# Graph network on one core: part of a histogram moved to ScalarE, one node stage reordered, another that makes its rows with TensorE

## What is computed

```python
x = _layernorm(x + _L2_gnn_ref(x, ...))          # its end: x1 = ln(x + agg); ln(x1 + gelu(x1 W1.T + b1) W2.T + b2)
def gat_conv(x, W, att_src, att_dst, b, src, dst):
    h = (x @ W).reshape(n, H, C)
    a_s = jnp.einsum('nhc,hc->nh', h, att_src)
    a_d = jnp.einsum('nhc,hc->nh', h, att_dst)
    ...                                          # softmax over each node's edges and the node itself
    out = jax.ops.segment_sum(h[s] * alpha[:, :, None], d, num_segments=n)
    return out.reshape(n, H * C) + b
h = gat_conv(x, W1, att_src1, att_dst1, b1, src, dst) + x @ Wsk1 + bsk1
h = jax.nn.relu(h)
out = gat_conv(h, W2, att_src2, att_dst2, b2, src, dst) + h @ Wsk2 + bsk2
```

## Time and profile before

| what | value |
|---|---|
| median of 3 runs | 4936.54 us (4929.94 to 4939.66) |
| the profiled execution: time, span | 4934.43 us, 4932.7 us |
| granted TensorE clock, mean over the span | 0.868 |
| PE, DVE, ACT, POOL busy | 3297.2, 3312.0, 2347.0, 3364.9 us |
| first walk | 71 to 378 us |
| third node stage | 2420 to 3164 us |
| fourth node stage | 3735 to 4209 us |

### The profile page before, as it was taken

One profiled execution on the slowest core, in us unless ns is written; L12 is line 12 of the kernel. 1 busy time (PEld: TensorE's weight loads), 2 busy tenths in 40 slices (PEclk: granted clock), 3 DMA queues, 4 the chain that ended last, 5 costly groups with the idle time before them and its releaser, 6 DMA issues. The chain is left out here.

```text
span 4932.7 us, 95098 instructions
## 1 busy us (share of the span) xinstructions
PE 3297.2 (67%) x20852; PEld 2470.8 (50%) x20853; DVE 3312.0 (67%) x13416; ACT 2347.0 (48%) x6751; POOL 3364.9 (68%) x4041
## 2 busy tenths in 40 slices
PE   0888868888886999767499999630005999321666
PEld 0776757777563444322267777420004777211665
DVE  6987874444785777789588888641805888624676
ACT  0556767767674444333288888400002444000566
POOL 3746757677455777457588888775674555674999
PEclk9999989999998999889799999855557999655888
DMA  4447869889897422101144444351116998441676
GB/s 96 150 142 234 256 194 265 245 253 266 255 284 246 149 53 52 30 28 39 63 143 145 145 145 145 109 152 41 37 41 210 293 294 270 113 111 51 194 224 199
DMA packets 592049, 784.40 MB, mean 159 GB/s; under 512 B 138298, under 2 KB 361838, under 8 KB 591298
## 3 DMA queue, kind: packets, MB, share of 16 engines
q1 hardware_dynamic: 430208, 532.17, 35.4%
q0 software_dynamic: 62848, 112.43, 9.4%
q10 hardware_dynamic: 98822, 138.05, 7.6%
HBM read 470.04 MB, written 317.95 MB: 160 GB/s over the span
## 5 line engine op out<-in xcount | busy, mean ns | idle before, releaser
L2895 POOL TENSOR_SCALAR n_hot<-node_of,d_krel 128x256 f32<-128x256 f32 x396 | 381.1, 978 | 65.2 <-ACTq L2951 65.2
L1374 ACT ACTIVATE n_r<-n_r,n_shift,n_rstd 128x128 f32<-128x128 f32 x784 | 321.6, 481 | 70.6 <-POOL n_shift L1365 65.7
L2923 PE MATMUL n_bank<-h_rows,n_hot 128*128 x1584 | 240.6, 320 | 145.7 <-POOL n_hot L2895 128.7
L2923 PEld LDWEIGHTS n_bank<-h_rows,n_hot 128*128 128x128 f32 x1584 | 228.2, 231 | 158.7 <-issue 158.6
L684 POOL DMA_INDIRECT agg<-e_whole,e_put_i x196 | 202.7, 1034 | 149.5 <-DVE e_whole L714 90.1
L1374 ACT ACTIVATE n_o<-n_y_ps,n_shift,n_rstd 128x128 f32<-128x128 f32 x784 | 292.7, 453 | 13.5 <-POOL n_shift L1645 13.1
L970 POOL DMA_INDIRECT by_src<-by_src_pay,by_src_place_i x196 | 207.7, 1060 | 116.4 <-DVE n_o L1552 59.5
L1000 POOL DMA_INDIRECT x_rows<-x,d_other_i x196 | 191.4, 976 | 117.6 <-POOLq L102 58.2
L615 POOL DMA_INDIRECT agg_dst<-e_rows,e_put_i x196 | 195.2, 996 | 102.0 <-issue 59.4
L2516 POOL TENSOR_TENSOR n_u<-n_u 128x512 f32<-128x512 f32 x98 | 124.5, 1270 | 205.4 <-DVE n_u L2463 205.4
L2645 POOL DMA_INDIRECT h_rows<-h,d_other_i x196 | 201.3, 1027 | 76.2 <-issue 59.4
(11 more groups left out here) (510 smaller groups left out, 11343.1 us busy)
## 6 DMA issues: line engine op xcount, KB each, us to landing
n_ag<-agg_dst SPq DMA_DIRECT2D x196, 264.0 KB
n_hs<-h SPq DMA_DIRECT2D x196, 264.0 KB
n_xs<-x SPq DMA_DIRECT2D x196, 256.0 KB, 4.2
agg_dst<-e_ev SPq DMA_DIRECT2D x196, 132.0 KB
y<-n_o ACTq DMA_DIRECT2D x98, 264.0 KB, 3.6
e1a_fed<-y SPq DMA_DIRECT2D x196, 132.0 KB
m<-e1a_ev SPq DMA_DIRECT2D x196, 132.0 KB
e1b_fed<-m SPq DMA_DIRECT2D x196, 132.0 KB
```

The source lines that it names most:

```text
L1374: ins = act.activation(out[:, g, 0:D], r[:, g, :], ACT.Identity, bias=shift[:, g:g + 1], scale=rstd[:, g:g + 1])
L2895: ins = pool.tensor_scalar(hot[:, i // STEPB % HOTS, i % STEPB, :], keep.node_of[:, :], e.krel[:, i:i + 1], None, ALU.is_equal)
L2923: ins = pe.matmul(bank[:, bass.ds(to + h * 256, SUMMED)], hot[:, s, k, h * P:(h + 1) * P], flat_rows[:, bass.ds(row, SUMMED)], start=False ...
```

## The change

Three edits, with no edge between them but the chain of stages.

First, the last 76 of the 196 digits are counted by ACT: the sum over a partition's edges of sign(key + level), once for each level, and the difference of two neighbouring sums, halved, is a count. DVE counts 120, and takes the differences.

```diff
+    def count_signs(self, act):
+        act.wait_ge(self.digits_found, 3)
+        for d in range(BY_SIGN):
+            if d >= FOUND:
+                act.wait_ge(self.signed, d - FOUND + 1)
+            act.activation(self.sign_of[:, d % FOUND, :], self.beside[:, HIGH:HIGH + J], ACT.Sign, bias=self.level[:, d:d + 1],
+                           accum_out=self.signs[:, d:d + 1]).then_inc(self.signed, 1)
...
-        for d in range(HIGH):
+        for d in range(HIGH - BY_SIGN):
...
-        dve.wait_ge(self.counted, HIGH)
+        dve.wait_ge(self.signed, BY_SIGN)
+        dve.wait_ge(self.counted, HIGH - BY_SIGN)
+        self.link(dve.tensor_tensor(self.hist[:, HIGH - BY_SIGN:HIGH], self.signs[:, 0:BY_SIGN], self.signs[:, 1:BY_SIGN + 1], ALU.subtract))
+        self.link(dve.tensor_scalar(self.hist[:, HIGH - BY_SIGN:HIGH], self.hist[:, HIGH - BY_SIGN:HIGH], 0.5, None, ALU.mult))
```

Second, the loops of the third node stage are written in another order, and `add_beta` runs two blocks later:

```diff
-                pipeline(pool, (4, deviation(1, sums2, rstd2)), (5, deviation(2, sums3, rstd3)), (1, deviation(0, sums1, rstd1)),
-                         (1, add_beta))
+                pipeline(pool, (3, add_beta), (4, deviation(1, sums2, rstd2)), (5, deviation(2, sums3, rstd3)),
+                         (1, deviation(0, sums1, rstd1)))
...
-                         (0, together(0, sums1)), (4, second_residual), (3, statistics(1, y_ready, lambda s: y_ps[s % BANKS])),
-                         (4, statistics(2, residual, lambda s: r2[:, s % 2])), (3, together(1, sums2)), (4, together(2, sums3)))
+                         (3, statistics(1, y_ready, lambda s: y_ps[s % BANKS])), (4, second_residual), (3, together(1, sums2)),
+                         (4, statistics(2, residual, lambda s: r2[:, s % 2])), (0, together(0, sums1)), (4, together(2, sums3)))
...
-                pipeline(pe, (2, turn1), (7, product3), (6, turn3), (3, ffn2), (2, ffn1))
+                pipeline(pe, (7, product3), (2, turn1), (6, turn3), (3, ffn2), (2, ffn1))
...
-                pipeline(act, (3, gelu), (2, move1), (5, third_norm), (6, move3), (1, first_norm), (7, keep_h))
+                pipeline(act, (3, gelu), (2, move1), (7, keep_h), (6, move3), (5, third_norm), (1, first_norm))
```

```diff
-        sp.dma_start(self.hs[:, s], block_rows(h, turn, s)).then_inc(self.h_in[s], 16)
...
-                pipeline(pool, (2, combine), (0, add))
+                pipeline(pool, (4, combine), (3, add))
...
-                pipeline(dve, (0, lambda turn, s: a.first(dve, turn, s)), (1, lambda turn, s: a.last(dve, turn, s)), (2, weigh), (4, total))
+                pipeline(dve, (2, lambda turn, s: a.first(dve, turn, s)), (3, lambda turn, s: a.last(dve, turn, s)), (4, weigh), (6, total))
...
-                pipeline(pe, (4, product), (3, residual), (0, turn_over))
+                def own_rows(turn, s):
+                    done(pe, moved, turn, s)
+                    bank_free(pe, a.own_kept, turn, s, 2)
+                    for g in range(GB):
+                        ins = pe.matmul(own_ps[g // 2][:, g % 2, :], xt[:, s, g, :], waug1[:, :], start=True, stop=True)
+                    ins.then_inc(own_ready[s], 1)
+
+                pipeline(pe, (6, product), (5, residual), (0, turn_over), (1, own_rows))
...
-                pipeline(act, (5, store), (0, lambda turn, s: a.exp(act, turn, s)), (4, keep_h), (3, relu), (0, move))
+                def keep_own(turn, s):
+                    done(act, own_ready, turn, s)
+                    free(act, a.u_ready, turn, s)
+                    for j in range(2):
+                        act.activation(hs[:, s, 2 * j:2 * j + 2, :], own_ps[j][:, :, :], ACT.Copy).then_inc(a.own_kept[s], 1)
+
+                pipeline(act, (7, store), (2, lambda turn, s: a.exp(act, turn, s)), (6, keep_h), (5, relu), (0, move), (1, keep_own))
```

More of the change, by code:

```diff
@@ L1078, in _ @@
                     by_source.keep_ends(act)
+                    by_source.count_signs(act)
                 for k in range(EV):
@@ L2401, in __init__, with load @@
         self.steps = [ph.sem(f"attend_steps{i}") for i in range(3)]
-        self.h_in, self.ag_in = slot_sems(ph, "h_in"), slot_sems(ph, "ag_in")
+        self.own_kept, self.ag_in = slot_sems(ph, "own_kept"), slot_sems(ph, "ag_in")
         self.less_ready, self.exps_ready, self.share_ready = (slot_sems(ph, n) for n in ("less_ready", "exps_ready", "share_ready"))
         self.u_ready = slot_sems(ph, "u_ready")
-    def load(self, sp, turn, s, used, h, agg):
+    def load(self, sp, turn, s, used, agg):
         sp.wait_ge(self.u_ready[s], used)
-        sp.dma_start(self.hs[:, s], block_rows(h, turn, s)).then_inc(self.h_in[s], 16)
         sp.dma_start(self.ag[:, s], block_rows(agg, turn, s)).then_inc(self.ag_in[s], 16)
@@ L2417, in first @@
         for k in (s - 1, s):
-            done(dve, a.h_in, turn, k, 16)
+            done(dve, a.own_kept, turn, k, 2)
             done(dve, a.ag_in, turn, k, 16)
@@ L2465, in weigh, with node_gat @@
                                     a.share[:, which, s].unsqueeze(3).broadcast_to([P, GB, GAT_HEADS, GAT_D]), ALU.mult)
-def node_gat(nc, keep, x3, h3, agg, one, two, s2, h2, a2):
+def node_gat(nc, keep, x3, agg, one, two, s2, h2, a2):
     with Phase(nc, "n3", freed="h_out product_ready r_ready share_ready exps_ready u_ready s_out turned added") as ph:
         wsk1, wsk2, wh, att = ph.sb("wsk1", [P, D]), ph.sb("wsk2", [P, D]), ph.sb("wh", [P, D]), ph.sb("att", [P, 2, D])
+        wh1, att1, waug1 = ph.sb("wh1", [P, D]), ph.sb("att1", [P, 2, D]), ph.sb("waug1", [P, ROW])
         waug, tmp, b1, b2 = ph.sb("waug", [P, ROW]), ph.sb("tmp", [P, D]), ph.sb("b1", [P, 2]), ph.sb("b2", [P, 2, D])
@@ L2480, in node_gat @@
         h_ps = [ph.ps(f"h_ps{j}", [P, 2, ROW]) for j in range(2)]
+        own_ps, own_ready = [ph.ps(f"own_ps{j}", [P, 2, ROW]) for j in range(2)], slot_sems(ph, "own_ready")
         weights, chain, w_ready = ph.sem("weights"), ph.sem("chain"), ph.sem("w_ready")
@@ L2488, in _ @@
             def _(sp):
-                for to, of in ((wsk1, one["Wsk"]), (wsk2, two["Wsk"]), (wh, two["W"])):
+                for to, of in ((wsk1, one["Wsk"]), (wsk2, two["Wsk"]), (wh, two["W"]), (wh1, one["W"])):
                     sp.dma_start(to[:, :], of).then_inc(weights, 16)
@@ L2492, in _ @@
                     sp.dma_start(att[:, i, :], two[n].rearrange("h c -> (h c)").partition_broadcast(P)).then_inc(weights, 16)
+                    sp.dma_start(att1[:, i, :], one[n].rearrange("h c -> (h c)").partition_broadcast(P)).then_inc(weights, 16)
                 for i, n in enumerate(("b", "bsk")):
@@ L2500, in load @@
                     sp.dma_start(xs[:, s], block_rows(x3, turn, s)).then_inc(x_in[s], 16)
-                    a.load(sp, turn, s, used, h3, agg)
+                    a.load(sp, turn, s, used, agg)
                 every_block(sp, load)
@@ L2524, in _ @@
                 attention_weights(dve, link, waug[:, :], wh[:, :], att[:, 0, :], att[:, 1, :], tmp[:, :])
+                attention_weights(dve, link, waug1[:, :], wh1[:, :], att1[:, 0, :], att1[:, 1, :], tmp[:, :])
                 link(dve.tensor_tensor(bias1[:, :], b1[:, 0:1], b1[:, 1:2], ALU.add))
```

11 lines of the change are left out of this document (8 added, 3 removed).

## The result

After the change the median is 4964.3 us (4960.4 to 4971.4, 6 runs) against 4936.2 us (4929.9 to 4942.2, 6 runs) before: ratio 1.0055, 95% interval 1.0045 to 1.0066, so 28 us slower. The profiled execution took 4962.0 us, its span is 4960.3 us at a granted clock of 0.867.

What follows compares the result with a forecast made beforehand. Bounds were DVE's serial count, a POOL-DVE ring in the third node stage and a PE-ACT ring in the fourth. Terms -19.5 - 7 + 39 = +12.5 us, added to the median, gave 4949 us, range 4905 to 4984.

Steps and rivals of the forecast that it cites:

- its own case: Whole kernel: the forecast of 4949 us, with its own range 4940 to 4962, chance 0.47.
- 21.1 - 0.8 - 1: Counting: 76 counts dropped from DVE save 21.1 us, less 0.8 for added steps and waiting, 1 for ACT finishing late.
- The estimate from the page of 349 ns a count: Counting: the Trainium skill's price for an ACT count without the read, 27 us for 76, hidden with 7 us to spare.
- 30 for the blocks, 9 for the start: Fourth node stage: 0.33 us more for each of 92 iterations, 30 us, plus 9 us for a later start; loss 39.
- The rival that the own rows cost PE nothing: Fourth node stage: it pays only its start, 9 us, for a total of 4919 us; chance 0.05.
- the ring itself gets shorter: Third node stage, POOL and DVE: together(1) no longer stands behind together(0) and statistics(2), some 1.1 us shorter.
- the middle of the four, 7.2: Third node stage: period from the ranges 6.9 to 7.2 and 7.1 to 7.5; gain 7 us, bounds 56 gained, 32 lost.
- meet almost exactly: Third node stage: second_residual begins 3.45 to 3.6 us after second_norm, add_beta 3.43, so one must wait for the other.
- do not run together: Third node stage: a DVE tensor_tensor with both inputs in SBUF and a POOL instruction exclude each other; 1.48 instead of 0.67 us.
- A third stage at PE's floor of 6.64: Third node stage: rival that the port leaves it alone, period 6.7, 56 us gained, total 4900; chance 0.25.
- `add_beta` winning always (7.6): Third node stage: rival that add_beta always goes first and POOL's power meets first_add, 32 us lost, total 4988; chance 0.15.
- the price of 0.74 us a count: Counting: rival that ACT's accumulator read is dear, 56 us for 76 counts, no gain, total 4968; chance 0.08.

Runs made afterwards that it cites:

- e3m_carry: Not a run: a matmul of PE just ahead of the fourth node stage, starting at 3570.0 us in the trace before and 3562.9 after.
- lags_only: Against the kernel before: only the longer lags of the fourth node stage, h3 still loaded, no own rows made; 4939.9 us, ratio 1.0003.
- own_twice: Kernel before with only the fourth node stage's change, its four own-row matmuls made twice in each block; 5059.2 us, ratio 1.0245 against before.
- order_only: Kernel before with only the third node stage's reordering, on all four engines; 4957.4 us, ratio 1.0032.
- dve_order: Kernel before with only DVE's new order in the third node stage, POOL, PE and ACT as before; 4997.8 us, ratio 1.0138.
- beta_later: order_only with POOL's add_beta behind deviation(1) instead of ahead of it; 4939.7 us, ratio 1.0013 against the kernel before.
- meet_again: residual_early with POOL's add_beta placed between deviation(2) and deviation(0); 4952.7 us, ratio 1.0031 against the kernel before.
- residual_early: order_only with one pair swapped on DVE, second_residual ahead of statistics(1); 4887.6 us, ratio 0.9890 against the kernel before.

## Why the prediction was right, and which term was not

The sign and the range of 4905 to 4984 held; 4964 lies just above the 4940 to 4962 that the forecast gave for its own case. The forecast was 12.5 us slower and the measurement 28. By stages of the trace, 1.8 of the 15 between them is the counting, 19 the third node stage, -4 the fourth and -1.6 the untouched stages. The third node stage's term had the wrong sign; that the sum's sign was right all the same is the fourth stage's size, and in this sense luck.

**Counting: the term holds in the trace.** Predicted 19.5 (its own terms, 21.1 - 0.8 - 1, make 19.3), and the sum at 108 to 112: it came at 111.7, 17.7 earlier. The runs of the counting alone gained 12. ACT's counts start 0.44 us apart, 0.45 estimated. The read was dearer than assumed (187 ns against DVE's 80), but it lies over the activations on both sides of it. The Trainium skill (ScalarE: Activation LUTs, section What ACT_TABLE_LOAD costs) gives 186 + 0.833 x 196 + 93 = 442 ns for the activation, which is what the trace shows. The estimate from the page of 349 ns a count, which has no read, came out too low: with the read between, the starts are 440 apart.

**Fourth node stage: the mechanism and nearly the size.** Predicted +39 (30 for the blocks, 9 for the start), measured +35 in the trace. From a bare iteration to the next the rise was 0.30 us (4.59 to 4.89), not 0.33. But the blocks before were not all 4.59 apart, and all 97 distances together grew by 24.7 us, not 30. The start cost 8.7, 9 predicted: the first product came 187.8 us after `e3m_carry` before and 196.5 after. `lags_only` puts 1.0 of that on the lags; the rest I put down to the own rows' weights and rounds, which was not parted. The last 1.7 of the 35 lie behind the last product. The rival that the own rows cost PE nothing is out: the busy share of weight loads, 77% before, read by the Trainium skill's rule (Perfetto Trace Analysis, section Identifying the Most-Contended Engine), leaves an estimated 1.08 us a block. The runs decide against that reading: of 0.90 us only 0.60 found room, `own_twice` shows that a further set costs its whole 0.90, and in the changed kernel PE has no wait although weight loads are busy for only 315.56 of 350 us, 90%.

**Third node stage: the step that failed.** I wrote "the ring itself gets shorter ... some 1.1 us", then "I take the middle of the four, 7.2", a gain of 7 us. Measured: a loss of 12. I had weighed one pair, `second_residual` with `add_beta`, and let a shorter ring pay. What sets the period is POOL's chain, whole. It can be written out for each kernel from the window's POOL busy time, the period P between `second_norm`'s starts, POOL's gaps between its own dependent steps (0.54 to 0.55 us a block in all of these traces) and its waits for `together(1)` and at the loop's end. A block's busy time is busy x P / 400. Without any meeting POOL's steps take 1.27 + 3 x 1.01 + 7 x 0.20 = 5.70 us; what steps took beyond these durations is the stretch. Busy time less stretch is 5.54 to 5.60 in all rows, not 5.70, since the records of neighbouring steps overlap a little. Busy and idle time make up P by construction, so the table proves nothing by adding up; what it shows is where the time lies, and that POOL is idle for nothing but its own gaps and the waits named.

| kernel | busy | of it stretch | + gaps | + waits | = P |
|---|---|---|---|---|---|
| before | 6.40 | 0.84 | 0.55 | 0.33 | 7.28 |
| only PE and ACT reordered | 6.41 | 0.85 | 0.55 | 0.23 | 7.18 |
| changed | 6.69 | 1.14 | 0.55 | 0.19 | 7.43 |
| `order_only` | 6.82 | 1.27 | 0.55 | 0.19 | 7.56 |
| `dve_order` | 6.60 | 1.03 | 0.55 | 0.81 | 7.96 |
| `beta_later` | 6.07 | 0.52 | 0.55 | 0.76 | 7.38 |
| `meet_again` | 6.86 | 1.27 | 0.55 | 0.06 | 7.47 |
| `residual_early` | 6.16 | 0.60 | 0.55 | 0.04 | 6.74 |

The first row has the answer to the 1.1 us: POOL waited only 0.33 us a block (18.0 us in 55 blocks), so with its steps as they were a shorter ring could give no more than that. Its stretches were 0.84, and the new order made them 1.14. The change gained 0.14 in waits and lost 0.29 in busy time, which is the 0.15 of the period. The two long ones that were to "meet almost exactly" overlapped in only one block of three. The new order of PE and ACT, which the sum had at nothing, gains 11 us when it stands alone. The Trainium skill (GPSIMD Engine Reference, section Key points) says that DVE instructions with two SBUF inputs contend with GpSimd, and these traces agree: in each of the eight, from 2600 to 3000 us, every stretched step of POOL (78 to 161 of them) lies over a DVE instruction with two SBUF inputs, and none over another kind alone. What it costs they add: a POOL step that comes second waits for the end of DVE's instruction, whatever its own size, so a 0.20 us step can pay 0.50 as a long one does. The other way round it holds for `add_beta` alone. The prediction's "do not run together" was too wide: in the trace before, 30 of the 88 powers that met `scale2` ran beside it with neither any longer.

**The rivals.** A third stage at PE's floor of 6.64 was given 0.25. It was not what the change did. With the pair swapped the stage does come to 6.74 and gained 53 us in the trace, near the 56 worked out, but by another way: meetings still add 0.60 us a block, POOL waits for no other engine (its list has 2.1 us in 400 behind its own issue), and PE, busy for 390 of 400, is not full. `add_beta` winning always (7.6) was not the case, since it won one block in six; that the reordering alone still came to 7.56 is due to the other stretches. The read of ACT's accumulator was dearer than assumed, but the price of 0.74 us a count did not come.

**Still open.** The runs of the counting alone show 12 us where its trace shows 19; the order of PE and ACT that gains 11 us by itself is not split further; and what the lower clock has of the losses of `dve_order` and `beta_later` was not measured.

## What to carry to other kernels

Write down the chain of the engine that is held up, block by block, as busy, stretched, gap and wait, before crediting a shorter ring: a ring shorter by 1.1 us is worth no more than the wait that it removes. Two loops that are each fixed meet at the same places again and again (here over a turn of six blocks), so one swap in one of them can be worth 1% of the kernel, and each order should be tried together with those of the engines that feed it. And a load that is hidden is worth nothing to remove: PE had room for 0.60 of the 0.90 us that four matmuls take, and the other 0.30 and a later start turned a hidden transfer into 35 us.

## What was not expected of the hardware

- An ACT count with a running sum shows as two records, 442 ns and a read of 187, that overlap: one every 440 ns, against DVE's 278 for the same 196 columns.
- A POOL step of 128x4 elements pays nearly as much beside a DVE instruction with two inputs in SBUF (0.20 to 0.70) as one of 128x512 (1.27 to 1.83). For the powers a tenth of a microsecond decides: before the change they took 1.59 to 1.60 us when `scale2` started 0.05 to 0.06 us behind them (58 times) and 1.01 when it started 0.15 behind (30 times).
- In `dve_order` the granted clock of the third stage fell to 0.93 while PE was busy for 351.79 of 400 us; in `order_only`, with 352.21, it stayed at 1.00. In the first, PE's waits for ACT's `n_r` came in 25 pieces, the longest of 2.0 us, in the other in 41, the longest of 1.6. The 0.93 is a mean of two levels: from 2614 to 2617, behind a wait of 1.87 us, the clock was at 0.50 (1.2 GHz), and from 2618 to 2630 at 1.00 (2.4 GHz). What of its 68 us the clock costs was not measured.
